# A decoder on one core: the scores in one run ahead of the turned probabilities

## The reference, cut to what matters

```python
def local_attention(q, k, v):                 # 16 heads of 64, windows of 32 tokens
    bk2, bv2 = (look(bk), look(bv))           # each window and the one before it
    sim = jnp.einsum('bhwie,bhwje->bhwij', bq, bk2) * QK_SCALE
    sim = jnp.where(mask, -jnp.finfo(sim.dtype).max, sim)
    attn = jax.nn.softmax(sim, -1)
    out = jnp.einsum('bhwij,bhwje->bhwie', attn, bv2)
...
for i in range(6):
    x = attn_layer(shift_tokens(x), Wqkv[i], q_scale[i], k_scale[i], Wo[i]) + x
    x = ffn_layer(shift_tokens(x), ln_g[i], ln_b[i], W1[i], b1[i], W2[i], b2[i]) + x
```

## Time and profile before

| what | value |
| --- | --- |
| median of 3 runs | 2076.47 us (2074.24 to 2077.68) |
| time of the profiled execution | 2077.16 us |
| its span, first to last instruction | 2075.4 us |
| what lies outside the span | 1.76 us |
| mean granted TensorE clock | 0.989 |
| PE busy | 1973.1 us (95% of the span) |
| DVE, ACT, POOL busy | 1407.7, 1393.9, 1086.2 us |

### The profile page before, as it was taken

How to read it: one execution, slowest core, us unless ns; L and a number is a source line. 1 busy time by engine, 2 the same in 40 slices (tenths; PEclk the granted TensorE clock), 3 DMA queues, 4 the chain that set the end, 5 groups by cost and what they waited for, 6 DMA issues and landing times.

```text
span 2075.4 us, 74512 instructions
## 1 busy us (share of the span) xinstructions
PE 1973.1 (95%) x32424; PEld 1171.9 (56%) x32424; DVE 1407.7 (68%) x1975; ACT 1393.9 (67%) x2125; POOL 1086.2 (52%) x709
## 2 busy tenths in 40 slices
PE   8989897789999999999999999999999999999997
PEld 5655654355555555555555655555555555555553
DVE  1454545677777777777777777777777787777762
ACT  5565564466777667776777677767776777677763
POOL 1000000496666666666666666666666666666650
PEclk9999998799999999999999999999999999999999
DMA  3000001132223222232222323222332223222220
GB/s 118 2 1 1 2 21 31 28 77 64 63 63 94 73 73 63 64 94 73 73 63 66 92 71 78 74 60 72 85 79 73 67 63 95 73 74 63 64 63 21
DMA packets 82210, 128.37 MB, mean 62 GB/s; under 512 B 17246, under 2 KB 28124, under 8 KB 81884
## 3 DMA queue, kind: packets, MB, share of 16 engines
q1 hardware_dynamic: 81884, 123.59, 22.9%
HBM read 21.81 MB, written 1.05 MB: 11 GB/s over the span
## 4 chain that ended last, share of the span: by engine, by line
PE 88%; ACT 5%; DVE 4%; issue 3%; DMA 0%; ACTq 0%; SPq 0%; DVEq 0%
PE ps L621 17%; PE ps L617 16%; PE ps L643 9%; PE ps L697 9%; PE ps L682 7%; PE ps L689 7%; PE ps L427 4%; PE ps L626 3%; PE ps L662 3%; PE ps L630 3%; DVE work L1254 2%; PE ps L523 2%; PE ps L441 1%; PE ps L655 1%; PE ps L650 1%
## 5 line engine op out<-in xcount | busy, mean ns | idle before, releaser
L1424 POOL TENSOR_TENSOR work<-work,RS 128x1024 f32<-128x1024 f32 x192 | 365.2, 1902 | 386.3 <-ACT RS L969 384.6
L1101 DVE TENSOR_TENSOR work<-ps,work 128x512 f32<-128x512 f32 (+1 forms) x288 | 247.7, 860 | 328.9 <-ACT work L1029 292.3
L621 PEld LDWEIGHTS ps<-ident,work 128*128 128x128 f32 x3072 | 342.8, 141 | 141.3 <-issue 104.7
L621 PE MATMUL ps<-ident,work 128*128 128x128 f32 x3072 | 394.2, 275 | 6.3 <-ACT work L997 2.4
L1443 POOL TENSOR_TENSOR work<-work 128x1024 f32<-128x1024 f32 x96 | 225.9, 2354 | 99.0 <-DVE work L1106 99.0
L1435 POOL TENSOR_TENSOR work<-work 128x1024 f32<-128x1024 f32 x96 | 227.2, 2367 | 69.1 <-DVE work L1106 69.1
L1106 DVE TENSOR_TENSOR work<-ps,work 128x512 f32<-128x512 f32 (+1 forms) x288 | 247.2, 858 | 0.0
L1041 ACT ACTIVATE work<-work 128x1024 f32<-128x1024 f32 x96 | 101.5, 1057 | 205.1 <-DVE work L1186 204.7
L1146 DVE TENSOR_REDUCE SS<-work 128x16 f32<-128x1024 f32 x192 | 232.0, 1208 | 0.0
L689 PEld LDWEIGHTS ps<-work 64*32 64x32 f32 x12288 | 134.8, 105 | 147.7 <-issue 132.9
L617 PE MATMUL ps<-WQ,XS 128*128 128x512 f32 x384 | 189.3, 616 | 8.0 <-issue 4.4
(11 more groups left out here) (184 smaller groups left out, 3091.8 us busy)
## 6 DMA issues: line engine op xcount, KB each, us to landing
work<-work SPq DMA_DIRECT2D x576, 128.0 KB
work<-work SPq DMA_DIRECT2D x336, 64.0 KB
WQ<-in_wqkv SPq DMA_DIRECT2D x6, 512.0 KB, 3.6
WK<-in_wqkv SPq DMA_DIRECT2D x6, 512.0 KB, 4.5
WV<-in_wqkv SPq DMA_DIRECT2D x6, 512.0 KB, 3.5
WO<-in_wo SPq DMA_DIRECT2D x6, 512.0 KB, 3.8
work<-ZR SPq DMA_DIRECT2D x48, 64.0 KB
W<-in_w SPq DMA_DIRECT2D x6, 341.0 KB, 3.2
```

The lines of the kernel that those rows point to most:

```text
L621: m = nc.tensor.transpose(flat(R)[:, t * 128:t * 128 + 128], src[:, t * 128:t * 128 + 128], ident[:, :])
L1101: V.tensor_tensor(h16(cos_part[:, j, cols]), h16(src), rotary_tabs[:, at:at + 64].unsqueeze(1).broadcast_to([PARTS, heads_in, 64]), ALU.mu ...
L1424: U.tensor_tensor(h16(qk_norm[:, j, :]), h16(cos_part[:, j, :]), inv_norms[:, j, :].unsqueeze(2).broadcast_to([PARTS, 16, 64]), ALU.mult). ...
```

## The change

The second half of the scores moves ahead of the turn of the probabilities, so that the 64 calls of the scores are one run; the signal `scores_ready` goes with the last of them. Nothing is added or taken away, and the other engines' programs are the same.

```diff
@@ -743,12 +743,10 @@
                     pe.wait_ge(mask_seeded, g)
                     if n == 3:
                         pe.wait_ge(keys_carried, (g + 1) // 4)
-                    scores(0, 4)
+                    scores(0, 8).then_inc(scores_ready, 1)
                 if c:
                     pe.wait_ge(probs_ready, g - 1)
                     turn(bank_z, probs[:, :, :, :].rearrange('p c a b -> p (c a b)')).then_inc(probs_turned, 1)
-                if b:
-                    scores(4, 8).then_inc(scores_ready, 1)
                 if f is not None and n == 0:
                     variance(f)
                 if f is not None and n == 1:
```

## The result

| | before | after |
| --- | --- | --- |
| median of 20 runs | 2077.22 us (2073.05 to 2082.17) | 2094.95 us (2082.59 to 2102.59) |
| span of the profiled execution | 2075.4 us | 2095.1 us |
| mean granted TensorE clock | 0.989 | 0.982 |

The ratio is 1.0085 [1.0075, 1.0096], 17.7 us slower. I had said slower as the likeliest, but by 4.6 us; the time lies above my range. The changed file is two lines shorter there: ACT's copy is now L1032, DVE's work on the keys L1104.

What follows compares the result with a forecast made beforehand. PE bounds the kernel, busy 95% of the span. Terms -12.9 (n = 1, 2), +1.3 (n = 0, 3), +13.1 (stalls), +2.6 (steps 2 to 5), +0.5 (weighing) sum to +4.6 us: 2081 us, range 2065 to 2092.

Steps and rivals of the forecast that it cites:

- steps 2 to 5: Early steps without a large piece as cover: longer stalls in 2 and 5, later weighing in 3 and 4; 2.6 us lost.
- the stalls from step 6 on: PE's waits at page ends grow as transposes move behind them: 13.1 us, plus 0.5 for page ends inside the weighing.
- Steps with n = 1 and 2: First score to first weighing, 4.52 to 4.19 us, ACT's copy covered; 0.33 us won in each of 39 steps, 12.9 us.
- the rival with a slow run: Scores: 128 small records without a break start more slowly, adding 11 us, giving 2092; chance 0.15.
- Steps with n = 0 and 3: First score to weighing: waiting for ACT's copy eats the gain; +0.04 us in each of 33 steps, 1.3 us lost.
- the stalls in the same steps: Sign in the profile after: PE's stalls stay in the same steps and program places, issue time growing from 11 to some 30 us.
- The six steps like 36: Steps 7, 16, 36, 60, 71, 80: page end within the scores, turn and copy no longer hidden in the stall; 6.9 us lost.
- 20, 31, 40, 51: Four steps with the page end inside the turn in the new order, splitting the wait; 2.4 us lost.
- 18, 38, 58: Stalled steps with n = 2, where the long piece covers the copy; 2.3 us lost.
- 27 and 91: With 29, steps whose page came 1 us before it was needed and would now stall; 2.0 us lost.
- SP's windows: Transfers of the values hold the DMA path, so a late page is usable 3.07 us after the first score regardless of PE.
- My rival, that no stall grows: Page ends: PE's request sets the packet's time, so reaching them sooner asks sooner; -10 us, 2066; chance 0.25.

Runs made afterwards that it cites:

- e2: New order with repeated work as padding, placing a page end in the scores' last quarter in every step with n = 0 and 2; 2135.24 us, ratio 1.0286.
- e4: Old order with padding that places a page end in the scores' last quarter in steps with n = 0 and 2; 2114.86 us, ratio 1.0194.
- e6: New order only in steps with n = 1 and 2 from step 6 on, old order elsewhere, no padding; 2068.26 us, ratio 0.9970.
- e10: Old order with the window transfers of the values, and the waits for them, left out from the third block on; 2070.17 us, ratio 0.9975.
- e5: New order from step 6 on, old order in steps 2 to 5, no padding; 2085.96 us, ratio 1.0046.
- e7: New order only in steps with n = 0 and 3 from step 6 on, old order elsewhere, no padding; 2090.73 us, ratio 1.0082.
- e9: New order with the window transfers of the values, and the waits for them, left out from the third block on; 2076.86 us, ratio 1.0008.
- e1: New order with repeated work as padding, keeping page ends out of the turn and the scores' last quarter from step 8; 2071.86 us, ratio 0.9979.
- e3: Old order with the padding meant to keep page ends clear of the scores' last quarter; 2074.12 us, ratio 0.9997.
- e13: New order in all steps from step 6 on, old order in steps 2 to 5, with the clear-page padding; 2065.88 us, ratio 0.9946.

## Why the prediction was wrong in size

The terms measured in the two traces add up to +20.3 where I had +4.6. Of the 15.7 us between, 7.5 lie in steps 2 to 5, 6.7 in the stalls from step 6 on and 3.0 in the copy with n = 0 and 3; the gain with n = 1 and 2 was 1.5 larger than forecast. The first two are the terms that failed.

- **Steps with n = 1 and 2**: forecast -12.9, measured -14.4. Right; the long run of scores is 1.41 us to the next row, near the 1.45 that I added up (0.66 + 0.79), so the rival with a slow run falls.
- **Steps with n = 0 and 3**: forecast +1.3, measured +4.3 to +4.6. Mechanism right: the copy ends last, 0.10 before the weighing. It is 0.10 a step and not 0.04, since with n = 3 the run of scores takes 1.50 us to the turn (1053.26 to 1054.76) and not 1.45.
- **`scores_ready`** is worth nothing: right. What lies between the weighing and the next values didn't move in ordinary steps.
- **The stalls from step 6 on**: forecast 13.1 + 0.5, measured 20.3. The claim that a late page's time stands still is right (3.40 and 3.35 us), and so is the price of what moves behind a page end (e2 against e4). In step 36 itself the page end lies after 104 scores in the new order and not 96, as the turn's 16 instructions moved behind it; PE is there at 1.1 us and not 0.93, which with a late page changes little. What failed is "the stalls in the same steps": that V and the windows settle which pages are late. The six steps like 36 were to lose 6.9 and lost 1.6, as the pages of 7, 16 and 36 came in time in this execution (the packets of 7, 16 and 36 lay 2.0 to 3.4 us ahead of the first score, and 0.5 to 1.0 behind it before); 20, 31, 40, 51 lost 3.0 (forecast 2.4); 18, 38, 58 3.0 (2.3); 82, 11, 62 0.8 (-0.5). But 27 and 91 lost 4.2, and 47 and 67, which the list doesn't have, 6.9: steps with n = 3 whose pages were in time before, at a page end that PE reached 2.0 to 2.3 us after the first score, and late now, until 3.1 to 3.4. The transposes had hidden no late page there; the page itself came earlier.
- **Which pages are late** is the step that failed in this term: seven changed places. Whether that is a draw or the order isn't settled. In the unpadded traces step 16's page is late in the old order at that step each time (before, e6, e10) and in time in the new one each time (after, e5, e7, e9). But in step 47 the old order has it in time before and late in e6 and e10, and the new one late in the changed kernel and in time in e5, e7 and e9. That the growth came out above 13 and not near it is thus in part luck. I had also taken stalled steps as the candidates. In before, after and e5 to e7 no page that ended within the first 93 scores of a step from 6 on was late; the candidates are the steps whose page ends behind that, n = 1 among them (49 and 89 waited in e5 and e6).
- **Half clock**: forecast nothing. In steps 47 and 67 it is what the growth has beyond the stall and the copy, 3.63 - 2.30 - 0.10 = 1.2 and 3.52 - 2.30 - 0.10 = 1.1 (2.30: from the last start before the stall to the first behind it). Step 27, with as long a wait and the whole clock behind it, grew by 2.36, stall and copy alone. This part lies inside the 20.3 and the 10.1.
- **Steps 2 to 5**: forecast +2.6, in the trace +10.1, by the medians 6 to 9. The largest term of the prediction that failed rests on "in 2 and 5 the stall grows by over 2 us, of which other engines' chains leave 1.2 each". The waits themselves grew by 0.7 (1.33 to 2.02) and 1.1 (1.53 to 2.67), and little of the rest was absorbed; to the stall came the copy's 1.16, and then half clock in the turn, the weighing and the queries, 1.8 us in the queries alone.
- **Why pages are late**: I put it down to SP's windows. By e9 and e10 they are at most some 0.4 us of it. My rival, that no stall grows because a run that gets to the page end sooner also asks sooner, falls for the late pages (1.90 us a wait against 0.96). For the share of late pages it isn't settled (n = 2 in e2 and e4).

The Trainium skill (Runtime: NRT & Kernel Launch, Instruction fetch mechanics) has the fetch at a block's end mostly hidden. Here the block of 256 agrees. The hiding does by count, with 16 or 17 late of some 220 page ends, and doesn't in the late part of a dense run of small matmuls: 20 more repeated calls in one step, which do little but move the page ends, cost 63 us (e1 and e2).

What stays open: why the request of a page waits for the small tiles, which pages come late and whether the order has a part in it (it changes between executions; the changed kernel's spread is 20 us, the old one's 9), and how much of the medians is half clock.

## What to carry to other kernels

Before moving a block of small matmuls, mark where PE's pages end (each 256 of its instructions, waits among them) and treat every end late in a dense run as a stall that may come (25 and 37 of some 44 did in e2 and e4), the ones that are in time today too: what stands ahead of the end covers it, what is moved behind it doesn't. Then judge an order with the page ends held out of the run's last quarter: here the same order is 17.7 us slower than the old one as the ends fall, and some 2 us faster with them held clear in both (e1 and e3). And apply a reorder only where its cover is long enough; two of four kinds of step carried the whole gain.

## What the hardware showed that I had not expected

- A wait of PE of 1.6 to 2.7 us can be followed by 3 to 10 us at the 1.2 GHz level: behind 2.02, 2.67, 2.08, 2.16 and 2.08 us in the changed kernel (steps 2, 5, 47, 60, 67). It happened in the old order as well: in e13, step 2, behind a wait of 1.60 us, the queries take 3.68 us:

```profile
422.30 0.43 PE L682 MATMUL ps<-KT,work 64*32 64x64 f32 x28 [1.60 <-issue]
...
423.37 3.68 PE L617 MATMUL ps<-WQ,XS 128*128 128x512 f32 x4
```

The length alone doesn't decide: in the changed kernel step 27 waits 2.05 us, as long as step 47, and the windows behind it have the whole clock:

```profile
852.00:856.00 4.00, 3.94 (x108) 2.16 (x110) 3.90 (x8) 1.77 (x4) 1.66 (x1) 1.00 0.02 4
```

- A late page of PE's instructions is usable some 3.4 us after the small work behind the keys begins (3.0 on an idle DMA path), and its packet is served 0.5 to 1.6 us after that work begins, though PE had begun the page before up to 5 us ahead of the packet. The same page of the program came 0.5 to 6.3 us ahead of the scores in another execution (steps 27, 47, 67 and 91 before).
